# Scores of a second attention layer: stacks of two F32R parts in the partitions' halves, in place of three bf16 parts in 96 rows

## The reference

```python
def taylor_exp(x):      # x: 16 features of one head
    x2 = (x[..., :, None] * x[..., None, :]).reshape(*x.shape[:-1], d * d) / r2
    return jnp.concatenate([ones, x / rrd, x2 / rd], axis=-1)
...
q = (hidden_states @ Wq.T)   # 16 heads x 16 features, k alike; v has 8 a head
A = jnp.tril(jnp.einsum('bhnd,bhmd->bhnm', taylor_exp(q), taylor_exp(k)))
y = jnp.einsum('bhnm,bhme->bhne', A, v)
z = 1.0 / (jnp.einsum('bhld,bhld->bhl', qf, jnp.cumsum(kf, axis=2)) + EPS)
s = (y * z) @ Wo.T
...
for _ in range(3):      # the gate: three coupled cycles of a small net
    tf = _coupling_net(out, ...)
    out = out + coupling * _twist(out)
x = x + s * silu(out)
```

## Time and profile before

| | |
|---|---|
| median of 3 runs | 995.53 us (991.98 to 997.0) |
| span of the profiled execution | 980.3 us (from the first to the last instruction; no other time of it is given) |
| median less span | 15.2 us |
| TensorE, ScalarE, VectorE, GpSimd busy | 894.9, 635.3, 695.6, 365.2 us |
| starts of the attention's blocks 0 to 7 | 701.7, 746.9, 779.6, 812.3, 844.9, 877.6, 910.3, 940.2 us |

### The profile page before, as it was taken

One profiled execution on the slowest core, in us unless ns is written; L12 is line 12 of the kernel. 1 busy time (PEld: TensorE's weight loads), 2 busy tenths in 40 slices (PEclk: granted clock), 3 DMA queues, 4 the chain that ended last, 5 costly groups with the idle time before them and its releaser, 6 DMA issues. The chain is left out here.

```text
span 980.3 us, 18388 instructions
## 1 busy us (share of the span) xinstructions
PE 894.9 (91%) x6674; PEld 459.3 (47%) x6674; DVE 695.6 (71%) x1054; ACT 635.3 (65%) x1380; POOL 365.2 (37%) x355
## 2 busy tenths in 40 slices
PE   4789999999999999989999989799679999999997
PEld 2233444343444444438888887322234444444443
DVE  6769888998989999803333358977857667766654
ACT  4458677778787878763233223476467778777875
POOL 4112021134443333004666631455636446644200
PEclk9569899999999999999999999999789999999999
DMA  7732526141404000016777562369987999999700
GB/s 225 258 151 89 187 100 222 40 161 46 180 22 180 28 26 25 3 51 202 210 220 218 165 200 69 80 104 141 137 90 75 100 119 100 104 101 115 88 12 22
DMA packets 80973, 114.30 MB, mean 117 GB/s; under 512 B 12946, under 2 KB 58004, under 8 KB 78452
## 3 DMA queue, kind: packets, MB, share of 16 engines
q1 hardware_dynamic: 73684, 94.87, 48.7%
q0 software_dynamic: 6352, 17.86, 5.3%
q10 hardware_dynamic: 848, 0.40, 0.1%
HBM read 56.00 MB, written 33.57 MB: 91 GB/s over the span
## 5 line engine op out<-in xcount | busy, mean ns | idle before, releaser
L985 DVE TENSOR_REDUCE a_nmax<-quad 128x2 f32<-128x1024 f32 x256 | 301.8, 1219 | 33.7 <-PE quad L596 31.5
L795 ACT ACTIVATE a_probs<-bank 128x512 f32<-128x512 f32 x339 | 190.9, 597 | 53.6 <-PE bank L613 36.3
L1867 ACT ACTIVATE a_late<-quad 128x256 f32<-128x256 f32 (+3 forms) x512 | 180.4, 461 | 37.6 <-PE quad L1636 36.8
L2021 DVE SCALAR_TENSOR_TENSOR a_late<-a_late,const 128x512 f32<-128x512 f32 x128 | 117.2, 923 | 74.6 <-ACT a_late L1867 74.2
L625 PE MATMUL av<-a_probs,a_va 128*32 128x256 f32 x2048 | 167.6, 400 | 0.9 <-ACT a_probs L795 0.6
L596 PE MATMUL quad<-k_stack,q_stack 24*128 24x512 f32 x512 | 133.0, 523 | 9.3 <-DVE a_nmax L985 5.0
L613 PE MATMUL bank<-q_stack,k_stack 26*128 26x512 f32 x339 | 137.1, 506 | 3.9 <-DMA q_stack<-a_nparts 2.5
L795 ACT ACTIVATE a_probs<-misc 128x512 f32<-128x512 f32 x173 | 103.2, 597 | 25.4 <-PE misc L613 13.9
L1636 PE MATMUL quad<-q_stack,k_stack 96*128 96x256 bf16 (+3 forms) x512 | 103.8, 303 | 7.8 <-ACT a_late L1867 4.0
L1647 PE MATMUL av<-a_late,a_va 128*32 128x512 f32 (+3 forms) x1024 | 96.3, 449 | 8.2 <-DVE a_late L2032 7.2
L504 POOL DMA_INDIRECT sorted_rows<-x_rows,a_slot x64 | 62.2, 972 | 104.2 <-PE av L625 101.7
(11 more groups left out here) (301 smaller groups left out, 1401.0 us busy)
## 6 DMA issues: line engine op xcount, KB each, us to landing
spread<-a_parts SPq DMA_DIRECT2D x48, 256.0 KB, 2.6
q_stack<-a_parts SPq DMA_DIRECT2D x96, 128.0 KB, 7.3
k_stack<-a_parts SPq DMA_DIRECT2D x96, 128.0 KB, 7.8
wu<-packed_weights SPq DMA_DIRECT2D x20, 384.0 KB, 3.7
m_wu<-packed_weights SPq DMA_DIRECT2D x19, 384.0 KB, 3.6
q_stack<-spread SPq DMA_DIRECT2D x7, 1024.0 KB, 5.0
k_stack<-spread SPq DMA_DIRECT2D x7, 1024.0 KB, 7.4
sorted_rows<-in_shape_constants POOLq DMA_DIRECT2D x5, 1040.0 KB, 5.5
```

The source lines that it names most:

```text
L795: act.activation(probs[:, (GH * s + j) % 8, :], col_bank(n)[:, :], ACT.Exp, scale=scale).then_inc(col_free, 1)
L985: dve.tensor_reduce(nmax[quad % 2][:, at:at + 2 * TT:TT], row_slot(n)[:, :, :], AX_X, ALU.max, negate=True)\
L1867: act.activation(probs[:, (64 * b + n) % 12, kt * P:T], quad[:, n % 4, kt * P:T], ACT.Square, bias=1.0, scale=0.25)\
L2021: dve.scalar_tensor_tensor(out=blocks, in0=blocks, scalar=1.0, in1=S["tri"][:, None, :].broadcast_to([P, GH, P]), op0=ALU.add, op1=ALU.mul ...
```

## The change

q and k are split in two F32R parts: ScalarE writes the first straight from PSUM (rounded by the write), VectorE the rest by one subtraction that reads PSUM again. GpSimd and the `full` and `rest` buffers have no share any more. Three pairings (`HALVES`) instead of six, 16 rows each: 48 rows. The weights of q and k are loaded so that the even heads' features lie in partitions 0 to 63 and the odd heads' in 64 to 127, and the stacks keep that: two heads, h and h + 1, lie side by side in the halves, each with 48 rows, and each score is an F32R matmul over the rows of one half. A transfer takes 64 partitions to 16, four heads of 512 fp32 each; 12 transfers a half as before. The bank of q_k is free only when VectorE has read it too. ScalarE waits for the part buffers in place of VectorE. `q_k` moves from steps 1, 2, 11, 12 to 1, 3, 11, 13.

```diff
-PAIRS = ((0, 0), (0, 1), (1, 0), (1, 1), (0, 2), (2, 0))
-KROWS = 96
 HALVES = ((0, 0), (0, 1), (1, 0))
+SIDE = P // 2
+KROWS = DQ1 * len(HALVES)
...
-                    src = io["L1_attn_" + name][k * P:(k + 1) * P, :].rearrange("(h d) c -> d h c", d=DQ1)
-                    sp.dma_start(w1[:, 2 * n + k, :], src).then_inc(loaded1, 16)
+                    src = io["L1_attn_" + name][k * P:(k + 1) * P, :].rearrange("(h e d) c -> e d h c", e=2, d=DQ1)
+                    for e in range(2):
+                        sp.dma_start(w1[SIDE * e:SIDE * (e + 1), 2 * n + k, :], src[e]).then_inc(loaded1, 16)
...
-        parts = [sb(f"parts{i}", [P, 3, T], BF16) for i in range(4)]
+        parts = [sb(f"parts{i}", [P, 2, T], F32R) for i in range(4)]
...
+        QK_AT = (1, 3, 11, 13)
...
-                heads = slice(8 * half, 8 * half + 8)
-                for n in rows:
-                    for op, (dst, part) in enumerate(((qs, PAIRS[n][0]), (ks, PAIRS[n][1]))):
-
-                        sp.dma_start(dst[par][DQ1 * n:DQ1 * (n + 1), heads, :], parts[2 * half + op][:, part, :]).then_inc(done, 16)
+                slots = slice(4 * half, 4 * half + 4)
+                for piece in pieces:
+                    n, e = piece // 2, piece % 2
+                    rows = slice(SIDE * e + DQ1 * n, SIDE * e + DQ1 * (n + 1))
+                    for op, dst in enumerate((qs, ks)):
+                        src = parts[2 * half + op][SIDE * e:SIDE * (e + 1), HALVES[n][op], :].bitcast(F32)
+                        sp.dma_start(dst[par][rows, slots, :], src).then_inc(done, 16)
...
-            def split_one(c, k):
...
-            for b in range(2, B):
-                split_one(4 * b, 0)
-                split_one(4 * b + 1, 1)
-                sum_earlier(b - 2, b % 2)
-                split_one(4 * b + 2, 2)
-                split_one(4 * b + 3, 3)
-            sum_earlier(B - 2, 0)
-            sum_earlier(B - 1, 1)
+            for b in range(B):
+                sum_earlier(b, b % 2)
...
-                wait(pe, qk_read, 4 * b + k)
+                wait(pe, split, 4 * b + k)
...
-                pe.matmul(quad[:, n % 4, kt * P:T], ks[par][:, h, kt * P:(kt + 1) * P], qs[par][:, h, kt * P:T],
-                          start=True, stop=True).then_inc(s_mm, 1)
+                at = slice(SIDE * (h % 2), SIDE * (h % 2) + KROWS)
+                pe.matmul(quad[:, n % 4, kt * P:T], ks[par][at, h // 2, kt * P:(kt + 1) * P].bitcast(F32R),
+                          qs[par][at, h // 2, kt * P:T].bitcast(F32R), start=True, stop=True).then_inc(s_mm, 1)
...
-                    if n <= 5 and t in (1, 2, 11, 12):
-                        q_k(i + 2, par, t - 1 if t < 8 else t - 9)
+                    if n <= 5 and t in QK_AT:
+                        q_k(i + 2, par, QK_AT.index(t))
...
-                wait(act, split, 4 * b + k - 1)
-                act.activation(full[op][:, :], (S["misc"] if b < 2 else misc2)[:, :], ACT.Copy).then_inc(qk_read, 1)
+                wait(act, stack_b if half else stack_a, STACK * b)
+                act.activation(parts[k][:, 0, :], (S["misc"] if b < 2 else misc2)[:, :], ACT.Copy).then_inc(qk_high, 1)
...
-            def cast(b, k):
-                half, op = k // 2, k % 2
-                wait(dve, qk_read, 4 * b + k + 1)
-
-                wait(dve, stack_b if half else stack_a, STACK * b)
-                dve.tensor_copy(parts[k][:, 0, :], full[op][:, :]).then_inc(qk_cast, 1)
+            def split_off(b, k):
+                wait(dve, qk_high, 4 * b + k + 1)
+                dve.tensor_tensor(parts[k][:, 1, :], (S["misc"] if b < 2 else misc2)[:, :], parts[k][:, 0, :], ALU.subtract).then_inc(split, 1)
```

More of the change, by code:

```diff
@@ L686, in turn_w1 @@
                 n = col_no["w1", k, 0]
-                pe.wait_ge(loaded1, 16 * 6)
+                pe.wait_ge(loaded1, 16 * 10)
                 wait(pe, col_free, n - 2)
@@ L1428, in sem @@
             return ctx.enter_context(nc.semaphore("a1_" + name))
-        full = [sb(f"full{i}", [P, T]) for i in range(2)]
-        rest = sb("rest", [P, T])
-        parts = [sb(f"parts{i}", [P, 3, T], BF16) for i in range(4)]
-        qs, ks = [q[0:KROWS] for q in S["qs"]], [k[0:KROWS] for k in S["ks"]]
+        parts = [sb(f"parts{i}", [P, 2, T], F32R) for i in range(4)]
+        qs, ks = ([a[:, :, :].rearrange("p h t -> p (h t)").bitcast(F32).rearrange("p (s t) -> p s t", s=H // 2) for a in S[name]]
+                  for name in ("qs", "ks"))
         va = [sb(f"va{i}", [P, TT, H, STRIP]) for i in range(2)]
@@ L1467, in second_layer @@
         zeroed, filled = sem("zeroed"), sem("filled")
-        qk_mm, qk_read, qk_cast = sem("qk_mm"), sem("qk_read"), sem("qk_cast")
-        rested, second, split = sem("rested"), sem("second"), sem("split")
+        qk_mm, qk_high, split = sem("qk_mm"), sem("qk_high"), sem("split")
         stack_a, stack_b = sem("stack_a"), sem("stack_b")
@@ L1492, in second_layer @@
         block = ctx.enter_context(nc.Block())
-        STACK = 16 * 2 * len(PAIRS)
+        STACK = 16 * 2 * 2 * len(HALVES)
+        QK_AT = (1, 3, 11, 13)
         EARLY = ((0, 1), (2,), (3,), (), (4, 5), (6,), (7,))
@@ L1514, in _, with stack @@
         def _(sp):
-            def stack(b, par, half, rows=range(len(PAIRS))):
+            def stack(b, par, half, pieces=range(2 * len(HALVES))):
                 done = stack_b if half else stack_a
@@ L1540, in _ @@
                 swap(n)
-                if B <= n < B + 2 * len(PAIRS):
-                    half, row = divmod(n - B, len(PAIRS))
-                    stack(0, 0, half, (row,))
+                if B <= n < B + 4 * len(HALVES):
+                    half, piece = divmod(n - B, 2 * len(HALVES))
+                    stack(0, 0, half, (piece,))
             stack(1, 1, 0)
@@ L1561, in _ @@
         def _(pool):
-            def split_one(c, k):
-                f, r, pt = full[k % 2], rest, parts[k]
-                wait(pool, qk_cast, c + 1)
-                wait(pool, split, c)
-                pool.tensor_tensor(r[:, :], f[:, :], pt[:, 0, :], ALU.subtract).then_inc(rested, 1)
-                pool.tensor_tensor(pt[:, 1, :], f[:, :], pt[:, 0, :], ALU.subtract).then_inc(second, 1)
-                wait(pool, rested, c + 1)
-                wait(pool, second, c + 1)
-                pool.tensor_tensor(pt[:, 2, :], r[:, :], pt[:, 1, :], ALU.subtract).then_inc(split, 1)
             def update(n):
@@ L1597, in _ @@
                         update(GROUP * (k - 1) + 2 * i + 1)
-                    for c in EARLY[k][i:i + 1]:
-                        split_one(c, c % 4)
-            for b in range(2, B):
-                split_one(4 * b, 0)
-                split_one(4 * b + 1, 1)
-                sum_earlier(b - 2, b % 2)
-                split_one(4 * b + 2, 2)
-                split_one(4 * b + 3, 3)
-            sum_earlier(B - 2, 0)
-            sum_earlier(B - 1, 1)
+            for b in range(B):
+                sum_earlier(b, b % 2)
         @block.tensor
@@ L1687, in turn_gate @@
                 wait(pe, gate_read, t)
-                wait(pe, qk_read, 8)
+                wait(pe, split, 8)
                 for m in range(TT):
@@ L1850, in read_qk @@
             def read_qk(b, k):
-                half, op = k // 2, k % 2
+                half = k // 2
                 wait(act, qk_mm, 4 * b + k + 1)
-                wait(act, split, 4 * b + k - 1)
-                act.activation(full[op][:, :], (S["misc"] if b < 2 else misc2)[:, :], ACT.Copy).then_inc(qk_read, 1)
+                wait(act, stack_b if half else stack_a, STACK * b)
+                act.activation(parts[k][:, 0, :], (S["misc"] if b < 2 else misc2)[:, :], ACT.Copy).then_inc(qk_high, 1)
             def squares(b, t):
@@ L1894, in main @@
                         read_o(i, par, 0)
-                    if n <= 5 and t in (1, 2, 11, 12):
-                        read_qk(i + 2, t - 1 if t < 8 else t - 9)
+                    if n <= 5 and t in QK_AT:
+                        read_qk(i + 2, QK_AT.index(t))
                     if t == 7 and n >= 1:
@@ L2066, in main @@
                         read_gate(t - 3)
-                    if n <= 5 and t in (1, 2, 11, 12):
-                        cast(i + 2, t - 1 if t < 8 else t - 9)
+                    if n <= 5 and t in QK_AT:
+                        split_off(i + 2, QK_AT.index(t))
                     if t in (4, 5) and n >= 1:
@@ L2091, in _ @@
                 if c in (2, 5):
-                    cast(0, c // 3)
+                    split_off(0, c // 3)
             dve.wait_ge(S["net_in"], S["net_loads"])
@@ L2131, in _ @@
                 for c in EARLY[n // GROUP + 1][n // 2 % 2:n // 2 % 2 + 1]:
-                    cast(c // 4, c % 4)
+                    split_off(c // 4, c % 4)
             for i in range(B):
```

1 line of the change is left out of this document (removed).

## The result

The changed kernel takes 1021.02 us (median of 4 runs, 1017.29 to 1021.65) where the kernel before takes 993.89 (4 runs, 991.98 to 997.0): a ratio of 1.026, 95% interval 1.0221 to 1.0298. That is 27 us slower. The forecast was 996, so no change, with 982 to 1011 as its range. It was wrong in size, and the largest single part came from something that no rival had in it, TensorE's clock.

What follows compares the result with a forecast made beforehand. It took TensorE to bound steps 4 to 7 and a loop of PSUM banks and ScalarE's squares the other stretches. Six blocks +1.8, blocks 6 and 7 -0.4, early part -1.0: +0.4 on 995.5, so 996 us, range 982 to 1011.

Steps and rivals of the forecast that it cites:

- The bound: Second attention's blocks: TensorE alone sets steps 4 to 7; elsewhere scores wait for PSUM banks that ScalarE's squares free.
- The stretch of steps 0 to 3: First four steps of a block: +0.1 us for the scores and +0.5 for the moved q_k.
- pairs 213 ns apart: Sign that would prove the forecast wrong: the two scores of a pair start 213 ns apart instead of together.
- steps 0 to 3 were over 7.9 us: Sign expected in the new profile: a block's first four steps take over 7.9 us.
- steps 4 to 7 under 8.3 us: Sign expected in the new profile: this stretch of a block, 8.67 us before, falls under 8.3.
- Steps 4 to 7 (TensorE alone): nearly all, -0.5 us: In the stretch where TensorE was busy throughout, nearly all of the pairs' 0.65 us saving a round counts.
- The three waiting stretches, "+0.1 each": Steps 0 to 3, 8 to 11, 12 to 15: savings of 0.1 twice, exposed weight loads +0.2, net +0.1 us each.
- the loop gets slower: Rival: exposed weight loads and moved q_k at their upper ends, +1 us a block, 8 in all, 1004; chance 0.2.
- Blocks 6 and 7, put at -0.2 each: Last two blocks, which have no q_k: -0.2 us each, -0.4 together.
- ScalarE stops on transfers: Rival: the layer loop's 8.2 us stop comes through whole, or ScalarE also stops at step 1: +6, 1002; chance 0.06.
- the early part: Layer loop: couplings resume about 2.5 us later, 3.5 us come back from slowed VectorE instructions; -1 us.
- a copy and three activations: Layer loop: ScalarE work of about 0.60 us each before VectorE goes on after the stop; couplings about 2.5 us later.

Runs made afterwards that it cites:

- b_qk13: Kernel before with q_k at steps 1, 3, 11, 13, nothing else changed: ratio 1.0025, blocks 1 to 5 at 33.11 us instead of 32.67.
- b_48of96: Kernel before with all its transfers, the score multiplying only rows 0 to 47 of 96: ratio 1.0157 to the kernel before.
- a_bf16: Changed kernel with bf16 parts and stacks instead of F32R, less exact, half the transfer bytes: ratio 0.9978 to the kernel before.
- a_qk12: Changed kernel with q_k back at steps 1, 2, 11, 12: ratio 1.0165 to the kernel before, block 6 at 30.42 us.
- a_late6: Changed kernel with the seventh q_k of the layer loop one slot later: ratio 1.022 to the kernel before, layer loop 86.3 us, not 92.6.
- a_fill: Changed kernel with added fp32 matmuls nobody reads before scores of steps 1, 9, 13, also 2 and 14 in blocks 6 and 7: ratio 1.0157 to before.
- b_8loads: Kernel before with the second layer's q and k weights loaded by eight transfers instead of four: ratio 0.9981 to the kernel before.
- a_onehalf: Changed kernel with every score taken from partitions 0 to 47, so no two heads run side by side: 1074.5 us, ratio 1.0915.

## Why the prediction was wrong, point by point

**The bound was read rightly, and the sign of the small terms too.** Pairs start within 4 ns, and 512 columns cost 0.66 us to the weigh where 0.64 was forecast. Masks take 0.69 us, the subtraction as well. Transfers moved 98 to 119 GB/s in the three stretches that they fill. ScalarE's copy and the weight loads cost 0. The stretch of steps 0 to 3 was put at +0.6 and measured +0.67. Of the signs that it named, pairs 213 ns apart did not come, and steps 0 to 3 were over 7.9 us as it said; "steps 4 to 7 under 8.3 us" did not come (8.59). The 115 and 119 GB/s of the short windows lie a little above the 109 that it worked out (a transfer to `out` falls in the one with 119); whole blocks have 99 to 103.

**"Steps 4 to 7 (TensorE alone): nearly all, -0.5 us" failed.** It measured -0.08. The saving of the pairs was sized rightly: -0.65 for a round, of which -0.32, -0.22 and -0.11 were to come in steps 4 to 6. By the starts of the scores they came to -0.21, -0.10 and -0.11, which are these, less 0.10 for the change of tile behind the transposes of steps 4 and 5. Step 7 then took 0.34: 0.10 for the change of tile ahead of step 8, 0.03 because four 128-column scores take 0.36 us even when nothing holds them (step 11), and 0.21 because the fourth waits for ScalarE's last square of step 6. So two terms were missing: 0.30 for three changes of tile, and a wait for a bank in a stretch that was counted as TensorE's alone.

**The three waiting stretches, "+0.1 each", came to +0.32, +0.24 and +0.07** when the order's own cost by `b_qk13` is taken off (+0.35 where +0.5 was forecast, +0.10 where 0 was). So the steady block is +1.0, not +0.3. Built up from the runs: 32.67 as before; +0.44 for the order (`b_qk13`); +0.68 for tiles of at most 64 rows (`b_48of96`, where no load is longer and no head paired); pairs in bf16, with what else the change takes off the other engines, bring it down to 32.56 (`a_bf16`), so together they are worth 1.2; F32R adds 1.1, its weight loads. The 1.2 is what is left when the terms are taken as independent, so that the sum comes out is no proof of it; in the changed kernel itself the order costs 0.3 and not 0.44. The terms were sized for one exposed load a step and none for the other tile. The pairs' gain was real and was paid back in the same steps. This is the rival "the loop gets slower", which asked for +1 a block and got it in blocks 1 to 5. Blocks 6 and 7, put at -0.2 each, have +0.45 of it (30.42 in `a_qk12` against 29.97, and taken to be the same in block 7). Together that is 5.9 of the 22.7 us.

**"ScalarE stops on transfers" had the place and the length right, and the sum wrong.** 8.2 us were forecast for the stop, 7.3 came, released by a transfer that landed 15.72 us after its issue. VectorE was freed as forecast (two products in 1.28 us, not 3.19). But the early part was put at -1 and measured +7.7. The transfer landed as far from the layer's start as before (76.0 us; 76.2 before), and the next coupling began 2.4 us later (2.5 forecast). But from the landing to block 0 it took 16.6 us in place of 8.7. Before, only VectorE stood, and ScalarE and TensorE went on with the layers meanwhile (690.60 above). Now the layers stood too, and had to be run one after another when the coupling behind them was due: it came at 715.48, 7.8 us after the first, where before 5.5 lay between the two. The step that failed is the one that counted a copy and three activations and not the matmuls between them, at 1.2 GHz: ScalarE waited 2.05 us (at 711.91) where it waited 1.18 before. `a_late6` without the stop is at +1.4.

**The clock was in no term.** Blocks 2 and 5 lose 1.2 us each, block 6 3.5 (from `a_qk12`'s 30.42) and block 7 by the same measure about 3.7: some 9.6 us together. With the 7.7 of the layer loop, the 5.9 of the loop in blocks 1 to 7 and the 0.6 that block 0 gives back, that is 22.6 of 22.7. The prediction had read a granted clock of 1.00 in the blocks and took it as fixed. That it was TensorE's own work that lowered it is shown twice: taking rows away from the scores of the kernel before lowers it in blocks 0, 6 and 7 (`b_48of96`), and adding full-height matmuls to the changed kernel restores it in blocks 1 to 6 (`a_fill`). In which block it falls no run explains.

**Open.** Whether the clock answers to the rows in use or to the height of the tile: 64 rows showed none of it in blocks 1 to 7 and as much as 48 in block 0, in one execution. Whether the matmuls that `a_fill` added help by their height or only by being more work was not tried either. How the 6.3 us of the layer loop divide between the stop and the clock after it stays open, and a kernel with two sets of part buffers, so that ScalarE needn't wait, wasn't tried. The 4 us ahead of the second layer are not explained: `b_8loads` excludes the loads, and runs of the kernel before alone spread over 10 us and more on a chip.

## What to carry to other kernels

Before packing heads into half-height tiles, count three things: how often the half-height tiles follow one of 128x128 (0.10 us each here, nothing behind the tiles of 128x32), whether the weights' type doubles their load (94 to 187 ns here), and whether the next score would have waited for its PSUM bank anyway, or will wait for it once TensorE is faster (step 7). The Trainium skill's page "TensorEngine Tiling (Array Packing)", section "Performance Considerations", warns that tiling doesn't speed up the emptying of PSUM; the 39 us of waits for ScalarE, unchanged, are that. And when a wait moves from one engine to another, ask what is queued behind it on its new engine, and follow it to TensorE: behind this stop of 7.3 us stood the layers, and TensorE's clock was at 1.2 GHz for the 34 us that followed.

## What was unexpected of the hardware

- The granted clock fell while TensorE's records were dense: 0.72 over a block in which it was busy 46.96 of 47.06 us with 48-row F32R scores one after the other (`a_onehalf`), and 0.88 in block 6 of the changed kernel, busy 33.34 of 33.95. With more work in the same block it was 1.00, and the block 2.8 us shorter.
- Scores over 48 and 64 rows cost the same, and scores over 80 and 96 rows too, with 0.68 us a block between them: 0.10 wherever they follow a tile of 128x128, and nothing where they follow one of 128x32.
- Two F32R matmuls in the two halves start 4 ns apart and share the time of one; the next pair follows after 0.335 us for 512 columns, in bf16 after 0.226.
